# Mixing in a fused kernel's dense stage as two 64-row products for each slice, one per batch, in place of one block-diagonal product

## The reference, cut to what matters

```python
x = x + conv(x)                                   # first stage of the kernel
x = x + einsum('bct,bcd->bdt', x, W1[cond])       # mixing: a 64x64 matrix per batch, 16 to choose from
x = x + x @ W2.T + bias2 + (x @ A2[ad].T) @ B2[ad].T      # dense, rank 16, 32 adapters
x = x + x @ W3.T + ((x @ A3[lab]) @ B3.T) * 0.5           # dense, rank 32, 5 labelers
```

## Time and profile before

| | |
|---|---|
| median of 3 runs | 1716.68 us (1714.7 to 1717.55) |
| the profiled execution's own time, which is its span | 1715.9 us |
| TensorE busy (products) | 1640.4 us, 96% |
| weight loads busy | 1552.5 us, 90% |
| VectorE, ScalarE, GpSimd busy | 51%, 25%, 35% |
| mean granted clock of TensorE | 0.987 |

### The profile page before, as it was taken

The page is one execution under the profiler, slowest core; times in us unless marked ns, Lnnn a source line. Parts: engine busy times, 40 slices in busy tenths (PEclk is TensorE's granted clock), DMA queues, the critical chain, the costliest instruction groups (busy, mean ns, idle before and its releaser), DMA issues.

```text
span 1715.9 us, 32079 instructions
## 1 busy us (share of the span) xinstructions
PE 1640.4 (96%) x10317; PEld 1552.5 (90%) x10317; DVE 870.9 (51%) x1501; ACT 436.0 (25%) x751; POOL 595.0 (35%) x769
## 2 busy tenths in 40 slices
PE   6889989999999997699999999999999999999999
PEld 5678878898889897699999999999999999999998
DVE  7851179999999999233333333333333333333332
ACT  3311144444444443111111111111111111111111
POOL 4541155666566665222222222222222222222221
PEclk9899999999999999899999999999999999999999
DMA  9401356666666664322223222322222222222221
GB/s 235 44 7 62 106 193 213 220 220 221 219 220 220 220 221 158 96 96 89 97 84 101 89 95 86 101 87 93 89 94 91 97 89 92 94 93 92 89 97 63
DMA packets 121163, 213.35 MB, mean 124 GB/s; under 512 B 57824, under 2 KB 74860, under 8 KB 118544
## 3 DMA queue, kind: packets, MB, share of 16 engines
q1 hardware_dynamic: 120842, 212.94, 38.7%
q10 hardware_dynamic: 294, 0.05, 0.0%
HBM read 140.61 MB, written 71.93 MB: 124 GB/s over the span
## 4 chain that ended last, share of the span: by engine, by line
PE 58%; POOL 0%; POOLq 0%; issue 0%; ACT 0%; DVE 0%; DVEq 0%
PE ps L1318 46%; PE ps L1292 7%; PE ps L1340 3%; PE ps L1306 1%; PE ps L1300 0%; POOLq L1147 0%; POOL dense L1168 0%; POOL m_gath L1149 0%; ACT dense L1200 0%; POOLq L1155 0%; POOLq L1154 0%; DVE y_out L1271 0%; POOL a_gath L1158 0%; POOL a_gath L1156 0%; POOL m_gath L1135 0%
## 5 line engine op out<-in xcount | busy, mean ns | idle before, releaser
L1318 PE MATMUL ps<-dense,x2t 128*128 128x384 f32 (+1 forms) x4608 | 823.7, 336 | 0.0
L1318 PEld LDWEIGHTS ps<-dense,x2t 128*128 128x128 f32 x4608 | 774.0, 188 | 11.5
L1168 POOL TENSOR_TENSOR dense<-a_gath,dense 128x384 fp32r<-128x384 f32 x128 | 126.6, 1011 | 520.2 <-ACT dense L1200 520.2
L1003 PE MATMUL ps<-toep,ut 128*128 128x512 f32 (+2 forms) x1152 | 229.3, 344 | 0.0
L1003 PEld LDWEIGHTS ps<-toep,ut 128*128 128x128 f32 x1152 | 196.2, 190 | 17.1
L479 POOL TENSOR_TENSOR toep<-toep_raw,toep 128x1024 fp32r<-128x1024 f32 x64 | 152.4, 2381 | 132.0 <-ACT toep L589 132.0
L1214 ACT ACTIVATE y_out<-ps 128x384 f32<-128x384 f32 x64 | 31.4, 491 | 566.7 <-PE ps L1340 566.7
L837 DVE COPY_PREDICATED xt<-mask,unfolded 128x512 f32<-128x512 uint8 x64 | 145.0, 2265 | 10.0 <-DVE unfolded L834 9.3
L1292 PE MATMUL ps<-m_gath,x_in 128*128 128x128 f32 x1024 | 128.1, 279 | 13.4 <-DMA x_in<-x_d 9.6
L1246 DVE COPY hm<-ps 64x128 f32<-64x128 f32 x64 | 18.1, 283 | 236.7 <-PE ps L1300 236.7
L1292 PEld LDWEIGHTS ps<-m_gath,x_in 128*128 128x128 f32 x1024 | 122.9, 196 | 13.9 <-DMA x_in<-x_d 9.8
(11 more groups left out here) (185 smaller groups left out, 1792.1 us busy)
## 6 DMA issues: line engine op xcount, KB each, us to landing
toep_raw<-kern_d SPq DMA_DIRECT2D x64, 512.0 KB, 4.2
xt<-in_x SPq DMA_DIRECT2D x64, 512.0 KB, 4.9
x_d<-xt SPq DMA_DIRECT2D x64, 512.0 KB, 2.7
x_in<-x_d SPq DMA_DIRECT2D x64, 512.0 KB, 3.6
out<-y_out SPq DMA_DIRECT2D x64, 512.0 KB, 2.7
stack<-b_d SPq DMA_DIRECT2D x128, 128.0 KB, 2.7
stack<-b_d SPq DMA_DIRECT2D x128, 64.0 KB, 2.7
w_raw<-in_L_cond_W SPq DMA_DIRECT2D x8, 512.0 KB, 7.1
```

What stands on the lines that cost most here:

```text
L1003: mm(y[:, half * HB + i * P:(half + 1) * HB], xs[:, a, half * half_t + i, :], tp[:, b, 0:HB - i * P], start=i == a == b == 0, stop=False)
L1168: ins = nc.gpsimd.tensor_tensor(to[:, 1], of, f(to[:, 0]), ALU.subtract)
L1318: ins = mm(outs[g], x2t[v][:, a, i, :], w[:, b, i % half_t, first:end], start=i == a == b == 0, stop=g == 2 and i == K8 - 1 and a == 1)
```

## The change

For each slice and each batch b there is now a product of its own: 64 rows of x1 (rows 0 to 63, or 64 to 127) by 128 columns as stationary operand, and the batch's 64x64 matrix streamed. Batch 0's results go to the first bank of `ps[0]`, batch 1's to the second, eight slices of 64 columns each. `m_gath` has 64 columns in place of 128 and needs no zeros, so two memsets and a semaphore go. VectorE's copy out of PSUM puts the two batches' columns side by side again, so that `x2f` is laid out as before.

```diff
--- before.py
+++ after.py
@@ -184,7 +184,7 @@
     x2t = pair("x2t", [P, 2, K8, P], F32R)
     y_out = pair("y_out", [P, T])
     a_gath = pair("a_gath", [P, K8, KR])
-    m_gath = pair("m_gath", [P, P])
+    m_gath = pair("m_gath", [P, C])
     c_gath = pair("c_gath", [KC, KR])
 
 
@@ -1062,7 +1062,6 @@
     y_ps, y_left, y_right = sem("y_ps"), sem("y_left"), sem("y_right")
     a_hi, a_lo = sem("a_hi"), sem("a_lo")
     tail_out = sem("tail_out")
-    gfixed = sem("gfixed")
     PAIRS = TILES // 2
     c_adapters = c_d[0:AR].rearrange("(a r) c -> a r c", r=R2)
     x1_rows = x1_d.rearrange("(n b) c t -> n (b c) t", b=2)
@@ -1132,10 +1131,7 @@
         @block.gpsimd
         def _(pool):
             for v in range(2):
-                nc.gpsimd.memset(m_gath[v][:], 0.0).then_inc(gfixed, 1)
-            for v in range(2):
                 nc.gpsimd.memset(c_gath[v][:], 0.0).then_inc(c_zeroed, 1)
-            pool.wait_ge(gfixed, 2)
             pool.wait_ge(c_zeroed, 2)
 
             def gather(k, v):
@@ -1146,7 +1142,7 @@
                 for b in range(2):
                     s = pool.value_load(index[0:1, bass.ds(2 * n + b, 1)], min_val=0, max_val=S1 - 1)
                     rows = slice(b * C, (b + 1) * C)
-                    ins = nc.gpsimd.tensor_copy(m_gath[v][rows, b * C:(b + 1) * C], mix[rows, bass.ds(s, 1), :].squeeze(1))
+                    ins = nc.gpsimd.tensor_copy(m_gath[v][rows], mix[rows, bass.ds(s, 1), :].squeeze(1))
                 ins.then_inc(gathered_m, 1)
                 pool.wait_ge(gathered_m, n + 1)
                 ready(pool, a_lo, n - 1)
@@ -1226,7 +1222,8 @@
                 n = 2 * k + v
                 dve.wait_ge(x2_ps, n + 1)
                 ready(dve, x2_lo, n - 1)
-                nc.vector.tensor_copy(x2f[v][:], ps[0][:].rearrange("p (i m) -> p i m", i=K8)).then_inc(x2_copied, 1)
+                nc.vector.tensor_copy(x2f[v][:].rearrange("p i (b d) -> p b i d", b=2),
+                                      ps[0][:].rearrange("p (b i d) -> p b i d", b=2, i=K8)).then_inc(x2_copied, 1)
                 dve.wait_ge(x2_hi, n + 1)
                 tt(x2t[v][:, 1], x2f[v][:], f(x2t[v][:, 0]), ALU.subtract).then_inc(x2_lo, 1)
 
@@ -1289,7 +1286,9 @@
                 pe.wait_ge(gathered_m, n + 1)
                 ready(pe, x2_copied, n)
                 for i in range(K8):
-                    ins = mm(ps[0][:, i * P:(i + 1) * P], x1_in[v][:, i * P:(i + 1) * P], m_gath[v][:], start=True, stop=True)
+                    for b in range(2):
+                        rows, to = slice(b * C, (b + 1) * C), b * HB + i * C
+                        ins = mm(ps[0][:, to:to + C], x1_in[v][rows, i * P:(i + 1) * P], m_gath[v][rows], start=True, stop=True)
                 ins.then_inc(x2_ps, 1)
 
             def turn(k, v):
```

## The result

The changed kernel takes 1742.05 us (median of 4 runs, 1740.78 to 1743.09) against 1717.12 for the kernel before (4 runs): a ratio of 1.0144, with a 95% interval of 1.013 to 1.0159. It is slower by 25 us, where 137 were forecast.

What follows compares the result with a forecast made beforehand. TensorE, busy 96% of the span, was taken as the bound; 62 x (1.79 + 0.36) = 133.3, + 3.9 - 0.4, gave +136.8 on 1715.9, with 0.8 to the median 1853.5 us; range 1807 to 1860, 8 in 10 down to 1736.

Steps and rivals of the forecast that it cites:

- loads in a queue: Mixing's 32 weight loads a tile follow one another, each setting a step: 1807 to 1860 us, chance 0.55.
- What bounds the kernel: Dense stage: TensorE is busy throughout and the chain over a tile runs through it alone, 15.68 us, mixing 1.79.
- load and stream are equally long: Mixing before the change: weight load and stream each fit the 0.111 us step and hide each other; only one is shortened.
- (1): Mixing: each of 16 products becomes two of 64 rows and 64 streamed columns; one's stream halves to 0.054 us.
- (2): Mixing: 32 loads a tile, not 16, still 128 columns wide; fewer rows make a load no cheaper.
- (3): Mixing: loads queue behind one another, 32 x 0.112 = 3.58 us against 1.79, so +1.79 us a tile.
- side by side rival: Mixing: loads of the two halves run beside each other, only the round trip is paid: 1739 us, chance 0.20.
- (4): Around mixing: setting the array to fewer rows and back costs 0.17 + 0.19 = 0.36 us a tile.
- (5): VectorE's copy from PSUM, 1.23 us now, reads and writes in another order; even twice as long it costs 0.
- (6): Start of the stage: GpSimd's gathers keep their size and two memsets go, -0.4 us.
- (7): Start: tile 1's mixing, 3.52 us at half clock, doubles for +3.5 us, and the round trip adds 0.4.
- The faster one: Mixing: halves side by side and 64-row loads no limit, a pair under 0.089 us: 1684 us, chance 0.08.

Runs made afterwards that it cites:

- pad_cols: The kernel before with its adapter product padded with zeros in columns only, 34 rows by 128 columns: 1722.58 us.

## Why the prediction was wrong, point by point

The sign was right and so were most terms; the size was not, because of the cases that the text had priced it took the wrong one for the likeliest: loads in a queue, +1.79 us a tile, where they ran in pairs and mixing grew by 0.14.

- **What bounds the kernel, and that load and stream are equally long** (first two parts): right. The run with half the stream kept the loads at 1.87 us and mixing at 1.73, and the one with full rows and 32 loads took 0.112 for each.
- **(1) and (2), half the stream, no cheaper load**: right. 64-row loads are recorded at 192 ns, and 0.112 is the step of a pair.
- **(3), loads queue behind one another, +1.79 us a tile**: this is the step that failed. They run in pairs, and mixing has 0.14 more in the chain, which is part of the round trip. The argument against the pairs was that in the trace of before no load starts ahead of the product before it. That was no evidence: in the dense stage of that kernel every product takes its rows from row 0 on, so neighbours always shared rows, and a pair had no occasion to show. With one half after the other most of the price of (3) is there: mixing 3.32 us against 3.58, the rest being the three or four loads at the seam. The Trainium skill says in TensorEngine Tiling, Key Properties, that different tiles load and multiply in parallel; the pair within 0.01 us agrees, and the prediction names that sentence for the side by side rival and left it at 0.20 against 0.55. In TensorE: Matmul & The Clock Gate, Step-by-step, it says that a load is pulled ahead if its row groups don't conflict; the overlap at the seam of the two halves, as read above, agrees with it.
- **(4), the round trip, 0.36 us a tile by the adapter product's row**: right, and nearly the whole result: 0.14 + 0.24 = 0.38 by the chain. It lies otherwise than the terms had it (0.17 and 0.19), more of it in the products behind. Taking it by the rows and not the columns was right too, as padding the one and the other shows. No handover between the halves is paid for: the step from pair to pair is 0.112, that of a full product.
- **(5) VectorE's copy**: 1224 ns as mean, 1225 before. Right.
- **(6), (7), the start**: tile 1's mixing takes 3.68 us in the chain, where 3.52 doubled was forecast, for the same reason as (3). The 48 products behind it take 9.39 and not 8.05: the granted clock stays at 0.50 up to 713.00, where before the change it was 1.00 from 712.90 on (the first fence is of the changed kernel, the second of the one before).

```profile
706.94 3.68 PE ps L1291 x32
710.62 9.39 PE ps L1317 x48
...
710.62:713.00 2.38, 2.38 (x9) 2.38 (x9) 1.23 (x1) 1.06 (x1) 0.00 (x0) 0.50 0.56 78
```

```profile
712.90:720.90 8.00, 8.00 (x51) 7.97 (x49) 3.02 (x5) 2.27 (x4) 2.20 (x3) 1.00 0.26 75
```

Against this mixing began 2.44 us earlier, at 706.94 and not 709.38; so the start gives -2.44 + 0.16 + 1.34 = -0.94, where +3.5 was forecast. The 0.4 us of the two memsets can't be seen in it: from GpSimd's first work to tile 1's mixing it is 11.19 us, as it was 11.21, and in the kernel before and in `pad_cols`, which begin alike, the first adapter product lies 2.3 us apart.

- **Rivals.** The side by side rival is what happened: 1739 worked out for it, 1742.05 measured. The faster one named the right condition, a pair in under 0.089 us, and the wrong way to it: not a load of fewer rows but one of fewer columns brings it. With four tiles, which is another kernel, the step for four is 0.058, and 1687.11 came out near the rival's 1684. The 0.74 ns a column that the prediction sets against this rival stands in none of its rows, which give 0.78 to 0.85.

Both halves in one PSUM bank wasn't tried. The Trainium skill, TensorEngine Tiling, Gotcha 1: PSUM Pressure, says that different row tiles can't use the same bank at the same time; no run here shows it, and what an order that allows for it would cost stays open.

## What to carry to other kernels

A product of few rows between full ones costs a round trip, here 0.36 us for 2 products of 34 rows and 0.38 for 32 of 64: pad it with zeros beyond 64 rows, as the 66 here, where its operands allow. To gather small products in one place may do as well; that wasn't tried. Before a stream is made shorter, look at whether the weight load beside it is as long; if it is, only a cut that shortens both pays, as the 64x64 tiles did here. And where a trace shows no overlap of two things, ask first whether it had any occasion to show it.

## What the runs showed that was not expected

- Two row halves that alternate pair up of themselves, without any order of the loads by hand: 32 loads in 1.86 us.
- A load runs ahead of several products that have not begun, if its rows are free: in the run with one half after the other some three or four of 32 overlap, by their spacing.
- In that run the granted clock falls to 0.50 in eleven of the tiles, though TensorE is never idle over 1000 to 1600 us; that costs 17 us. The kernels with pairs, with four tiles and with full rows have 1.00 there.
- Four tiles of 64 by 64 run side by side with plain fp32 operands: 64 loads in 1.02 us.
